# Values copied out of PSUM in one piece of 128 rows, blocks of 32 tokens paired 0/2 and 1/3, and a new order of the steps

## The reference

```python
for i in range(6):
    x = attn_layer(shift_tokens(x), ...) + x      # shift: half of the channels come from the token before
    x = ffn_layer(shift_tokens(x), ...) + x
return x0 + x

def attn_layer(x, Wqkv, qs, ksc, Wo):
    q, k, v = split(x @ Wqkv)                     # 16 heads of 64
    q = l2norm(q) * qs;  k = l2norm(k) * ksc      # then the rotary terms, by cos and sin
    # each window of 32 queries sees its own 32 keys and the 32 keys before it
    sim = einsum('bhwie,bhwje->bhwij', bq, bk2) * 8
    out = einsum('bhwij,bhwje->bhwie', softmax(where(mask, -big, sim)), bv2)
    return out @ Wo

def ffn_layer(x, ...):                            # layer norm, 128 -> 2 * 341, a * gelu(gate), 341 -> 128
```

## Time and profile before

| | us |
|---|---|
| median of 3 runs (lowest, highest) | 4047.65 (4046.55, 4050.84) |
| the profiled execution | 4048.09 |
| its span, first to last instruction | 4046.3 |
| PE, DVE, ACT, POOL busy | 3729.9, 3487.8, 3422.3, 2387.8 |
| mean granted TensorE clock | 0.982 of full speed |

### The profile page before, as it was taken

The page is one execution under the profiler, slowest core; times in us unless marked ns, Lnnn a source line. Parts: engine busy times, 40 slices in busy tenths (PEclk is TensorE's granted clock), DMA queues, the critical chain, the costliest instruction groups (busy, mean ns, idle before and its releaser), DMA issues.

```text
span 4046.3 us, 125302 instructions
## 1 busy us (share of the span) xinstructions
PE 3729.9 (92%) x49248; PEld 2338.2 (58%) x49248; DVE 3487.8 (86%) x7192; ACT 3422.3 (85%) x9269; POOL 2387.8 (59%) x1420
## 2 busy tenths in 40 slices
PE   5999999967999999999999999999999999998987
PEld 2444444434666666666666666666666666666665
DVE  6999999957889898888988888898898888888884
ACT  3999999956888888888888888888888888888885
POOL 2434443436666666666666666666666666666662
PEclk7999999988999999999999999999999999999998
DMA  1000001002333333333333333333343333433332
GB/s 50 8 9 9 9 9 36 1 0 50 80 76 77 90 85 81 75 80 86 87 82 74 80 77 95 85 77 77 76 98 80 79 76 75 98 82 79 76 82 56
DMA packets 158791, 263.19 MB, mean 65 GB/s; under 512 B 45696, under 2 KB 72064, under 8 KB 157952
## 3 DMA queue, kind: packets, MB, share of 16 engines
q1 hardware_dynamic: 158208, 255.20, 26.8%
HBM read 26.43 MB, written 2.10 MB: 7 GB/s over the span
## 4 chain that ended last, share of the span: by engine, by line
PE 62%; DVE 18%; ACT 12%; issue 3%; POOL 2%; SPq 1%; DMA 1%; DVEq 0%; POOLq 0%; ACTq 0%
PE ps L655 17%; ACT arena L931 6%; PE ps L601 5%; PE ps L596 5%; PE ps L688 5%; PE ps L724 5%; PE ps L542 4%; PE ps L733 4%; PE ps L762 3%; PE ps L709 3%; PE ps L768 3%; DVE ssq L1164 3%; PE ps L537 3%; PE ps L775 3%; DVE arena L1147 2%
## 5 line engine op out<-in xcount | busy, mean ns | idle before, releaser
L655 PE MATMUL ps<-WB,arena 128*128 128x512 f32 x2304 | 1110.5, 605 | 132.5 <-DVE arena L1244 61.4
L931 ACT ACTIVATE arena<-arena,nmx 128x64 f32<-128x64 f32 x3072 | 1020.1, 337 | 4.4 <-DVE arena L1222 3.8
L475 POOL TENSOR_TENSOR arena<-arena 128x1024 f32<-128x1024 f32 x192 | 454.4, 2367 | 516.3 <-DVE arena L1147 516.0
L655 PEld LDWEIGHTS ps<-WB,arena 128*128 128x128 f32 x2304 | 399.9, 192 | 463.2 <-issue 438.8
L907 ACT ACTIVATE arena<-ps 128x1024 f32<-128x1024 f32 x384 | 393.5, 1025 | 314.1 <-PE ps L655 307.7
L491 POOL TENSOR_TENSOR arena<-arena,rinv 128x1024 f32<-128x1024 f32 x192 | 365.2, 1902 | 389.9 <-DVE rinv L1195 389.9
L931 ACT ACTIVATION_READ_ACCUMULATOR arena<-arena,nmx 128x1 f32 x3072 | 584.3, 190 | 0.0
L1141 DVE TENSOR_TENSOR arena<-ps,tables 128x1024 f32<-128x1024 f32 x384 | 464.7, 1210 | 87.4 <-ACT arena L907 87.4
L688 PEld LDWEIGHTS ps<-ident,arena 128*128 128x128 f32 x3072 | 355.6, 141 | 239.1 <-issue 173.6
L1147 DVE TENSOR_TENSOR arena<-ps,tables 128x512 f32<-128x512 f32 x768 | 489.9, 678 | 0.0
L480 POOL TENSOR_TENSOR arena<-arena 128x1024 f32<-128x1024 f32 x192 | 455.1, 2371 | 30.8 <-DVE arena L1147 30.8
(11 more groups left out here) (109 smaller groups left out, 6675.9 us busy)
## 6 DMA issues: line engine op xcount, KB each, us to landing
arena<-arena SPq DMA_DIRECT2D x768, 128.0 KB, 2.3
arena<-arena SPq DMA_DIRECT2D x1536, 64.0 KB
WB<-wb SPq DMA_DIRECT2D x24, 512.0 KB, 5.0
arena<-X SPq DMA_DIRECT2D x384, 32.0 KB, 1.9
arena<-Y SPq DMA_DIRECT2D x96, 128.0 KB, 2.4
arena<-wa SPq DMA_DIRECT2D x8, 581.0 KB, 3.8
WF<-wf SPq DMA_DIRECT2D x6, 537.5 KB, 4.5
keep<-xT SPq DMA_DIRECT2D x1, 2048.0 KB, 7.8
```

Of the source, the lines that this page charges most:

```text
L475: pool.tensor_tensor(tu[:, K], t1[:, K], t2[:, K], ALU.add).then_inc(addk_r, 1)
L655: i = pe.matmul(banks[:, c, :], xs_[t % RING], WB[:, w * INNER + c * COL:w * INNER + (c + 1) * COL], start=True, stop=True)
L931: i = act.activation(pe3[:, :, h, :], sc[:, 64 * h:64 * h + 64].rearrange("p (k q) -> p k q", k=2), ACT.Exp, bias=nmx[:, h:h + 1], accum_o ...
```

## The change

`values` becomes one instruction over 128 rows into side 1. Windows 1 and 3 find their keys' windows there as they lie (rows 0 to 127 are windows 0 to 3), and side 0, for windows 0 and 2, is side 1 moved by one window: one DMA of 96 rows and one of 32 rows from the tile before. `widen` places its eight pieces for the new pairing, and `outputs` writes them back in order of tokens. The DMAs of `vshift` for tile s-1 are issued in stage s (before: for tile s in stage s). The loops start one stage earlier and LAG is 13; the added stages hold no work. The order of steps changes on every engine. The core of the diff:

```diff
 SP   widen:  o = (WIN * w + 96) % P;  side w % 2 in place of w // 2
      def vshift(t):
          sp.wait_ge(v_r, t + 1)
-         need(sp, vs_in, 16 * PARTS * t)
-         for dst, side, src, row, held in ((64, 0, (t - 1) % RING, 96, 1), (96, 0, r, 0, 0), (0, 1, r, 32, 0),
-                                           (32, 1, r, 64, 1)):
-             sp.dma_start(vv[r][dst:dst + WIN, side, :], vv[src][row:row + WIN, held, :])
+         need(sp, vs_in, 32 * t)
+         sp.dma_start(vv[r][0:96, 0, :], vv[r][0:96, 1, :])
+         sp.dma_start(vv[r][96:P, 0, :], vv[(t - 1) % RING][96:P, 1, :])
 ACT
-    def values(t, side):
-        if side == 0:
-            act.wait_ge(v_mm, t + 1)
-            need(act, vs_in, 16 * PARTS * t)
-        rows = slice(64 * side, 64 * side + 64)
-        i = act.activation(vv[t % RING][rows, side, :], kv_ps[rows]..., ACT.Copy)
+    def values(t):
+        act.wait_ge(v_mm, t + 1)
+        need(act, vs_in, 32 * (t - 1))
+        act.activation(vv[t % RING][:, 1, :], kv_ps..., ACT.Copy).then_inc(v_r, 1)
...
```

More of the change, by code:

```diff
@@ L41 @@
 FF = TILES // PER
-LAG = 12
+LAG = 13
 NEG = -1.0e30
@@ L389, in _ @@
                 sp.wait_ge(x_done[u], NB * (BLOCKS + 2) + 1)
[L390 to L394, removed]
+            for s in range(-3, TILES + LAG):
+                if live(s + 1):
+                    xs(s + 1)
+                if chunk(s, 7) is not None:
+                    ff_in(chunk(s, 7))
                 if live(s - 2):
                     widen(s - 2)
-                if new and (s + 2) % NT == 0:
-                    keys_in(l)
-                    queries_in(l)
+                if live(s - 1):
+                    vshift(s - 1)
+                if live(s + 2) and (s + 2) // NT > 0 and (s + 2) % NT == 0:
+                    keys_in((s + 2) // NT)
+                    queries_in((s + 2) // NT)
                 if 0 < (s + 1) // NT < LAYERS and (s + 1) % NT == 0:
@@ L405, in _ @@
                     hidden_in((s - 7) // NT)
[L406 to L409, removed]
                 q = chunk(s, 11)
@@ L502, in ff_rstd @@
                 pool.tensor_tensor(rstd[:, 0, :], ve[:, 0, :], power[:, 0:4], ALU.pow).then_inc(frs_r, 1)
-            for s in range(-2, TILES + LAG):
+            for s in range(-3, TILES + LAG):
+                if live(s):
+                    unit_q(s)
                 if live(s + 1):
@@ L513, in _ @@
                 if live(s + 1):
-                    unit_q(s + 1)
+                    unit_k(s + 1)
         @block.tensor
@@ L964, in _ @@
             keys_on(0)
-            for s in range(-2, TILES + LAG):
+            for s in range(-3, TILES + LAG):
                 if live(s + 1):
                     square(s + 1, kv_ps, K, k_mm, sqk_r)
+                    square(s + 1, q_ps, Q, q_mm, sqq_r)
                 if live(s):
                     turned_k(s)
-                if live(s + 1):
-                    square(s + 1, q_ps, Q, q_mm, sqq_r)
+                if live(s - 1):
+                    exponents(s - 1, range(0, 4))
                 if live(s):
@@ L981, in _ @@
                 if live(s):
-                    values(s, 0)
+                    values(s)
+                if chunk(s, 8) is not None:
+                    ff_norm(chunk(s, 8))
                 if chunk(s, 9) is not None:
                     ff_gelu(chunk(s, 9), 1)
[L985 to L988, removed]
+                if 0 < s + 1 < TILES:
+                    keys_on(s + 1)
                 if chunk(s, 9) is not None:
@@ L1290, in _ @@
                 if chunk(s, 9) is not None:
-                    ff_hidden(chunk(s, 9), 1)
+                    ff_hidden(chunk(s, 9), 0)
                 if chunk(s, 10) is not None:
                     ff_final(chunk(s, 10))
+                if live(s):
+                    masked(s)
+                if chunk(s, 7) is not None:
+                    ff_unit(chunk(s, 7))
+                if chunk(s, 9) is not None:
+                    ff_hidden(chunk(s, 9), 1)
                 if live(s):
@@ L1297, in _ @@
                     ff_hidden(chunk(s, 9), 2)
-                if chunk(s, 7) is not None:
-                    ff_unit(chunk(s, 7))
                 q = chunk(s, 11)
```

78 lines of the change are left out of this document (36 added, 42 removed).

## The result

The changed kernel takes 4150.36 us (median of 5 runs, 4125.68 to 4152.82), the kernel before 4050.84 on the same chip (median of 5, 4046.55 to 4051.36). The ratio is 1.0236, with a 95% interval of 1.021 to 1.0261. The prediction was 4056 with a range up to 4092: wrong, by about 94 us. The profiled execution is the shortest of the five (4125.68), so that its rows show 77.6 us of the 99.5 between the medians.

The account below looks back on a forecast made before the run. PE was taken as nearly the bound, busy 60.0 of 63.8 us a group. 48 groups x (0.54 lost in D - 0.37 won before G) = +8 us on 4048.1 gave 4056, with an 8-in-10 range of 4000 to 4092.

Parts of the forecast that it names:

- `ff_stats` is no longer held: Stage T, DVE: its last instruction, formerly held by POOL's `unit_k`, takes 0.17 us in place of 0.75.
- `norms` are held 0.9 by `ff_rstd`: Stage T, DVE: `norms` waits 0.9 us for POOL's `ff_rstd`, so B's queries start at 17.35.
- the rival without the hold: Stage T: `norms` runs freely beside `ff_rstd`, B's queries start at 16.45, G at 28.3: 4013 us, chance 0.29.
- Tokens at 29.1: Stage B, SP: `xs` lands at 29.1 us after T's start, so G starts at 29.2 in place of 29.57.
- tokens late: Start of G: keys wait for `xs` behind the 384 KB DMA, G at 30.2: 48 us more, 4104; chance 0.16.
- `scores` waits 0.54 for `turned_q`: Stage D: table load and four exponentials ahead of `turned_q` end it at 9.3, PE wants `scores` at 8.78.
- G runs without a wait: Stage G, PE: no wait; `exponents` end some 0.3 us later, covered by `attend`; effect nothing.
- The change saves ACT only: Last rival: one `values` piece saves ACT 1.0 us, but G starts at 29.57 as ever: 4074 us, chance 0.06.

Follow-up runs that it names:

- xs_early: The changed kernel with `xs` one tile ahead again and first in the stage: 4075.80 us.
- vshift_small: The changed kernel with `vshift` moving 64 of the 1024 columns from the fourth tile on: 4072.62 us.
- vshift_first: xs_early with `vshift(s-1)` ahead of `ff_in` and `widen`: 4031.82 us.
- warm_pe_old: warm with the old order of PE and ACT in the first half of a stage: 4105.12 us.
- pair_dve: pair_only with DVE's new order and `ff_rstd` ahead of `unit_k` on POOL: 4010.06 us.
- sp_old: vshift_first with `xs` moved to right behind `vshift`, SP's whole order as before: 4022.91 us.
- exps_late: The changed kernel with `turned_q` ahead of all exponentials: 4251.42 us.
- dve_only: The kernel before with DVE's new order and `ff_rstd` ahead of `unit_k` on POOL: 4015.75 us.
- pair_only: The kernel before with the new pairing alone (one values copy, two DMAs), all orders as before: 4046.84 us.
- pair_pe: pair_only with the new order of PE and ACT in the first half of a stage: 4126.70 us.
- warm: sp_old with a one-column exponential as ACT's last instruction in each G stage, so the table loads there: 3986.83 us.

## Why the prediction was wrong, step by step

- **`ff_stats` is no longer held: right.** 0.17 (0.169 to 0.172) in all 37 cases from 1200 to 3600 us; before, the mean of 38 was 0.754.
- **`norms` are held 0.9 by `ff_rstd`: wrong.** L1178 takes 0.192 in the mean of 147 stages, as in 151 of before, and `ff_rstd` lies beside it in one of four. The queries of B start at 16.17; the forecast had 17.35, the rival without the hold 16.45. That rival's mechanism was right, its 4013 was not. L1180, `nwt<-nwt,ssc`, takes 0.192 in the mean of 37 cases beside `ff_rstd` and in the mean of 110 without it. The Trainium skill, "SBUF — State Buffer", section "Who interferes with whom", would have a DVE instruction with two SBUF inputs (such as L1180) wait for POOL to end; the measurement decides against it here.
- **Tokens at 29.1: the term of the sum that was mis-sized.** The prediction bounded the landing by 28.8 and 30.2, 2.6 and 4.0 after the first issue of `xs`, and took 2.9. Measured are 3.96 in the group shown and 4.56 in the median of the 29 waits, above the upper bound. As the issue itself came 0.6 earlier than forecast, G starts at 29.54 in the group shown and all that B had won is gone. The rival "tokens late" had the place and the mechanism. It left unpriced that B waits for its own tokens too ("if T or D are touched too, more"), and that is the larger half: 21.6 us of the 40.0. All of it is 1.08 us a group, 52 us over 48. xs_early prices the whole at 75 us, against 48 in the rival. The stated range ended at 4092, although the prediction's own later landing gives 4104.
- **D: `scores` waits 0.54 for `turned_q`: right.** 19.4 us in 37 waits are 0.52 each, 25 us over 48 groups; the prediction's own terms (9.3 less 8.78) give 0.52 too. Taking the load away gave 36 us.
- **G runs without a wait: nearly right.** What PE waits between G's keys and D's is 0.28 us a group, nearly all of it issue.
- **Idle time for issue was put at nothing: the step that cost most.** It grew by 63 us in 2400, 1.71 us a group or 82 us over 48, more than any term of the sum. A row for it stood in the waits of before (22.8, `attend`), and the prediction never mentions it. The DMA records show what it is: PE waits for its next 16 KB of instructions. About 30 of the 63 follow the bytes of `vshift` (vshift_small, vshift_first), and most of the rest goes with PE's old order (warm_pe_old, and pair_dve beside sp_old). Why the packet comes late for one order and in time for another stays open.
- **Half clock was not in the sum.** PE is busy for 30 us more on the same work, and of the kernels above the slowest has the most windows below full clock (exps_late, 38), while dve_only has none. How much each wait adds through the clock is not separated.
- **"The change saves ACT only": right where it is alone** (pair_only), though not by its 4074, since the loss came with the orders.

In steps of medians: after 4150.4, `xs` early 4075.8, `vshift` ahead of `widen` 4031.8, and ahead of `xs` 4022.9, the table loaded in G 3986.8. So the order on SP cost some 120 us (the last 9 of 127 are not clear of noise) and the place of the load 36. What remains is a gain of 61 to 64, as one takes the before runs beside it or the first ones, of which DVE's order with PE's old one gives 32 to 38 (dve_only, pair_dve).

## What to carry to other kernels

An order of steps is one thing across all engines: early queries on PE need the early `ff_unit` on DVE, and half of such a change can be slower than none of it (pair_pe) and than all of it (warm_pe_old against warm). When a load loses its slack, take the landing time behind the largest transfer ahead of it, not the median of quiet issues; here 4.56 and not 2.0. Price a long stall on PE (here 3.15 us) above its length, and leave out no row of the waits because it has no releaser: lay its ends beside the packets that bring the instructions.

## What the hardware showed that was not expected

- PE's idle time put down to issue ends 1.1 to 1.6 us after a 16 KB packet of its instructions has come, in 772 of 802 cases. The same work in another order has 27.5 or 90.4 us of it in 2400.
- The load of an activation table (1.28 us) stands ahead of the first instruction that needs it. One exponential of one column (0.20 us) at a place where ACT is idle moves it there: 36 us over 48 groups.
- One DMA of 384 KB within SBUF in place of three of 128 KB costs 31 us in 192 tiles, with more idle time of PE for issue (93.6 against 72.6).
- POOL's `unit_k` (1.90 us, 128x1024) held a small DVE instruction from 0.17 to 0.75; POOL's power on 128x4 (1.02 us) held nothing.
- After PE stood for 3.15 us, a pair of products took 2.08 us in place of 1.12.
